# TensorE's completion reports in a graph kernel: on the last matmul, or on a drain behind it

## The reference

```python
# GCN, three times: z1 = conv(x), z2 = conv(z1), z3 = conv(z2)
xw = einsum('ni,tio->tno', x, W)                 # one product per edge type
x_j = xw[edge_type, col] * norm[:, None]         # gather one row per edge, scale it
out = segment_sum(x_j, row, num_segments=N) + b  # add it to the edge's node
z = leaky_relu(out, 0.01)
# GAT, once
alpha = leaky_relu(a_src[src] + a_dst[dst], 0.2)
e = exp(alpha - segment_max(alpha, dst)[dst])
msg = (e / segment_sum(e, dst)[dst])[:, :, None] * xp[src]   # gather again
out = segment_sum(msg, dst)
```

## Time and profile before

| | |
|---|---|
| Time, median of 3 runs | 11929.52 us (11923.69 to 11931.49) |
| Span of the profiled execution (the page gives no other time of it) | 11925.3 us |
| Busy: PE, PEld | 5307.0 us (45%), 4105.0 us (34%) |
| Busy: DVE, ACT | 4574.2 us (38%), 3992.0 us (33%) |
| Busy: POOL | 6395.8 us (54%) |
| First gather of GCN, last gather of GCN | 691.5 us, 8375.1 us |
| First gather of GAT, last gather of GAT | 8505.5 us, 11826.8 us |
| DMA share | 0.1 to 0.2 of the 16 engines |

### The profile page before, as it was taken

The page is one execution under the profiler, slowest core; times in us unless marked ns, Lnnn a source line. Parts: engine busy times, 40 slices in busy tenths (PEclk is TensorE's granted clock), DMA queues, the critical chain, the costliest instruction groups (busy, mean ns, idle before and its releaser), DMA issues.

```text
span 11925.3 us, 149378 instructions
## 1 busy us (share of the span) xinstructions
PE 5307.0 (45%) x32765; PEld 4105.0 (34%) x32766; DVE 4574.2 (38%) x12940; ACT 3992.0 (33%) x12236; POOL 6395.8 (54%) x6521
## 2 busy tenths in 40 slices
PE   5843434434533434343433434343444444444444
PEld 4632322223322323232322323232344444444444
DVE  9952222222322212222322222222555555555556
ACT  6522222222322222222322222222455454445455
POOL 1656566565456565656466565656344444444443
PEclk9975655656655655565655556555566666666666
DMA  1011111111221111111211111111122222222222
GB/s 47 35 42 43 41 44 43 41 44 41 65 55 44 40 44 40 44 40 44 76 42 44 40 44 40 44 40 44 49 69 70 68 71 69 69 68 69 70 69 65
DMA packets 432687, 612.42 MB, mean 51 GB/s; under 512 B 232038, under 2 KB 249491, under 8 KB 432539
## 3 DMA queue, kind: packets, MB, share of 16 engines
q0 software_dynamic: 208832, 428.96, 13.7%
q1 hardware_dynamic: 223707, 182.02, 4.6%
HBM read 437.29 MB, written 51.28 MB: 41 GB/s over the span
## 4 chain that ended last, share of the span: by engine, by line
another core or an unknown queue 48%; DVE 16%; issue 15%; PE 8%; ACTq 5%; DVEq 4%; ACT 3%; POOL 0%; DMA 0%; POOLq 0%; SPq 0%
DVEq L1604 3%; PE bank L1196 3%; ACT g_step L912 3%; ACTq L896 2%; DVE a_miss L1717 2%; PE wide L1196 2%; DVE g_hot L1620 2%; ACTq L912 1%; DVE acc L1634 1%; DVE a_max L1722 1%; DVE lo_hot L1262 1%; DVE acc L1788 1%; PE bank L1191 1%; DVE v_hot L1387 1%
## 5 line engine op out<-in xcount | busy, mean ns | idle before, releaser
L737 POOL DMA_INDIRECT g_rows<-gcn_table,rec_idx x4743 | 4487.1, 946 | 2894.2 <-ACT g_step L912 1484.6
L912 ACT ACTIVATE g_step<-g_rows,rec_w 128x128 f32 x5580 | 1791.5, 390 | 5679.7 <-remote 4618.4
L762 POOL DMA_INDIRECT a_roll<-gat_table,src_plane x1612 | 1524.6, 946 | 1801.0 <-ACT a_cand L937 1375.4
L1634 DVE TENSOR_TENSOR acc<-acc,bank 128x512 f32 x930 | 637.9, 686 | 3828.8 <-remote 3238.9
L1191 PE MATMUL bank<-zeros 1*128 1x512 bf16 x930 | 490.9, 528 | 2909.9 <-DVE acc L1634 2104.6
L1196 PE MATMUL bank<-g_step,g_hot 128*128 128x128 f32 x7440 | 1621.7, 386 | 128.4 <-issue 50.6
L1196 PEld LDWEIGHTS bank<-g_step,g_hot 128*128 128x128 f32 x7440 | 1391.8, 280 | 487.9 <-issue 487.9
L1222 PE MATMUL bank<-a_msg,a_hot 128*128 128x130 f32 x3608 | 798.9, 389 | 1648.7 <-DVE a_msg L1768 1635.0
L1222 PEld LDWEIGHTS bank<-a_msg,a_hot 128*128 128x128 f32 x3608 | 685.6, 283 | 1786.3 <-DVE a_msg L1768 1452.3
L1191 PEld LDWEIGHTS bank<-zeros 1*128 1x128 bf16 x930 | 89.9, 97 | 3099.0 <-DVE acc L1634 2163.3
L937 ACT ACTIVATE a_cand<-a_miss,a_rows 128x128 f32<-128x128 bf16 x3608 | 1095.9, 386 | 14.9 <-DMA a_rows<-a_roll 8.8
(11 more groups left out here) (272 smaller groups left out, 5880.3 us busy)
## 6 DMA issues: line engine op xcount, KB each, us to landing
a_rows<-a_roll SPq DMA_DIRECT2D x451, 264.0 KB
g_rows<-gcn_table,rec_idx POOLq DMA_INDIRECT x4743
gcn_table<-rows SPq DMA_DIRECT2D x147, 256.0 KB
a_roll<-gat_table,src_plane POOLq DMA_INDIRECT x1612
e_dst<-by_dst_dst SPq DMA_DIRECT2D x451, 2.0 KB
gat_table<-acc SPq DMA_DIRECT2D x7, 462.0 KB
out_x<-xs SPq DMA_DIRECT2D x6, 448.0 KB
gcn_slots<-nothing SPq DMA_DIRECT2D x4, 468.0 KB, 6.8
```

The costliest lines, as they stand in the source:

```text
L737: pool.indirect_dma_start(out=g_rows[:, tile % RING, :], out_offset=None, in_=gcn_tables[layer % 2], in_offset=bass.IndirectOffsetOnAxis(a ...
L762: pool.indirect_dma_start(out=a_roll[:, g % ROLL, t, :], out_offset=None, in_=gat_table, in_offset=bass.IndirectOffsetOnAxis(ap=src_plane[ ...
L912: last = nc.scalar.activation(g_step[:, j, k, :].unsqueeze(1), g_rows[:, bass.ds(slots[k], 1), :], ACT.Copy, scale=rec_w[:, bass.ds(q.at(0 ...
L1634: V.tensor_tensor(dst_ap, dst_ap, sums_of(j).rearrange("p (k d) -> p k d", k=GP), ALU.add).then_inc(s_gadd, 1)
```

## The change

First, in the two loops PE no longer adds to `s_gpe`, `sa["T"]`, `sa["pv"]` and `sa["node"]` with the last matmul of each batch. A drain instruction stands behind it, and the drain adds to the semaphore. A drain ends when the engine has finished everything ahead of it. Reports of other matmuls (table products, transposes between layers, the sort) stay on the matmuls.

Second, numbers that are compared with a semaphore are loaded by themselves, with a check that they lie in their range: on ACT the landed tile, on SP the landed group and the slot.

```diff
@@ SP, GAT
-                    _, (tile, slot) = nc.values_load_multi_w_load_instructions(
-                        gat_at[0:1, bass.ds(q.at(0), 1), :].rearrange("p g k -> p (g k)"),
-                        engines=(mybir.EngineType.SP,), min_val=0, max_val=GAT_GROUPS - 1,
-                        skip_runtime_bounds_check_because="a step less the begun blocks, at most the last group")
-                    slot = nc.s_assert_within(slot, 0, ROLL - 1,
-                                              skip_runtime_bounds_check_because="a group modulo the ring")
+                    tile = sp.value_load(gat_at[0:1, bass.ds(q.at(0), 1), 0], min_val=0, max_val=GAT_GROUPS - 1)
+                    slot = sp.value_load(gat_at[0:1, bass.ds(q.at(0), 1), 1], min_val=0, max_val=ROLL - 1)
@@ ACT, GCN
                 def slots_of(q):
+                    tile = act.value_load(gcn_at[32:33, bass.ds(q.at(0), 1), GP], min_val=0,
+                                          max_val=CH * CCOLS - 1)
                     _, values = nc.values_load_multi_w_load_instructions(
-                        gcn_at[32:33, bass.ds(q.at(0), 1), :].rearrange("p g k -> p (g k)"),
-                        engines=(mybir.EngineType.Activation,), min_val=0, max_val=CH * CCOLS - 1,
-                        skip_runtime_bounds_check_because="a step less the begun blocks, at most the last tile")
-                    return values
+                        gcn_at[32:33, bass.ds(q.at(0), 1), 0:GP].rearrange("p g k -> p (g k)"),
+                        engines=(mybir.EngineType.Activation,), min_val=0, max_val=RING - 1,
+                        skip_runtime_bounds_check_because="a tile modulo the ring")
+                    return *values, tile
...
@@ PE, GCN: sum of a group
                                                 g_step[:, j % 3, k, :], start=False, stop=(k == GP - 1))
-                    last.then_inc(s_gpe, 1)
+                    pe.drain().then_inc(s_gpe, 1)
@@ PE, GAT: transposes
-                    last.then_inc(sa["T"], 1)
+                    pe.drain().then_inc(sa["T"], 1)
@@ PE, GAT: messages
-                    last.then_inc(sa["pv"], 1)
+                    pe.drain().then_inc(sa["pv"], 1)
@@ PE, GAT: node values
-                    last.then_inc(sa["node"], 1)
+                    pe.drain().then_inc(sa["node"], 1)
```

More of the change, by code:

```diff
@@ L895, in slots_of @@
                 def slots_of(q):
+                    tile = act.value_load(gcn_at[32:33, bass.ds(q.at(0), 1), GP], min_val=0,
+                                          max_val=CH * CCOLS - 1)
                     _, values = nc.values_load_multi_w_load_instructions(
-                        gcn_at[32:33, bass.ds(q.at(0), 1), :].rearrange("p g k -> p (g k)"),
-                        engines=(mybir.EngineType.Activation,), min_val=0, max_val=CH * CCOLS - 1,
-                        skip_runtime_bounds_check_because="a step less the begun blocks, at most the last tile")
-                    return values
+                        gcn_at[32:33, bass.ds(q.at(0), 1), 0:GP].rearrange("p g k -> p (g k)"),
+                        engines=(mybir.EngineType.Activation,), min_val=0, max_val=RING - 1,
+                        skip_runtime_bounds_check_because="a tile modulo the ring")
+                    return *values, tile
                 def scale(q, values):
                     j = q.slot(0) % 3
-                    *found, tile = values
-                    slots = [nc.s_assert_within(v, 0, RING - 1,
-                                                skip_runtime_bounds_check_because="a tile modulo the ring")
-                             for v in found]
+                    *slots, tile = values
                     if q.live(-3) or layer:
```

## The result

The changed kernel took 12783.45 us (median of 4 runs, 12781.1 to 12819.33), the kernel before 11926.6 us (4 runs, 11923.29 to 11931.49): a ratio of 1.0728, with a 95% interval from 1.0713 to 1.0743. The forecast was 9290 us. The change made the kernel slower by 857 us.

A forecast was written before the change was run, and what follows sets the result against it. It took PE's reports, held while gathers are in flight, to bound the kernel. 11925.3 - 1485 (GCN) + 45 (batches at layer ends) - 1200 (GAT) = 9285, so 9290 us for the median; range 9140 to 12,100.

The forecast's parts named there:

- What bounds the kernel now: GCN and GAT gather loops: PE's reports are held while gathers are in flight; DVE and ACT idle over 4600 us each.
- the circle: Gather loops: POOL gathers until its ring fills, reports held; after it stops they come, ACT scales, slots free, POOL gathers again.
- my sum: Gather loops after release: GCN loses POOL's 1484.6 us of waiting for ACT; GAT takes 2120 us, a gain of 1200.
- If a drain's report is sent at once, the circle breaks: Drains in both loops: each loop then runs at its slowest engine's pace; full release had chance 0.68, at 9290 us.
- its sign of being wrong in this way: Gather loops: "remote" waits as long as now, with drains many us long while POOL gathers.
- My argument against this rival: GCN, against the drain being held too: three held reports arrive one right behind another, as if queued and ready.
- The drain is held as well, slower: Rival, chance 0.12: drain and PE stand while the report is held; GCN +1100 to +1700 us, GAT +400, time 13,700.
- ACT's second load ... the gathers hide it: ACT in GCN: net 0.45 us a group, at most 2.9 us in all, hidden below POOL's 4.34 us.
- SP's loads, "nothing": SP's second load: about 0.6 us a step, ahead of waits ending 5 us apart, so no cost.
- A sequencer's addition is not held there: GCN, against a rival (0.11) of reports late whoever sends: ACT, needing POOL's `s_land`, starts 0.1 us after DVE.

The follow-up runs named there:

- Set 2: Four kernels on chip 15 (kernel before 8942.95 us): one load 8943.18 us, narrow gathers 9130.51, plain copies 8462.06, waiting for landed gathers 11818.26.
- silent drain: Changed kernel with the four reports back on the last matmul and a drain that reports nothing behind each batch: 12810.32 us, 1.0736 of the kernel before.
- set 1: The change taken apart on chip 14 (kernel before 11931.05 us): loads alone 12185.93 us, with GCN drains 12705.49, with GAT drains 12263.69, report plus drain 12810.32.
- set 3: Repeats on chip 11 (kernel before 11921.82 us): changed kernel 12776.21 us, ACT's five numbers in one load with reports on matmuls 11953.2, plain copies 9756.59.
- landing wait after each four: Changed kernel, POOL waiting after each run of four GCN gathers until they have landed: 13058.56 us on chip 8, 11818.26 on chip 15.
- loads only: Changed kernel with all four reports back on the last matmul, leaving only the range-checked loads: 12185.93 us, 1.0215 of the kernel before.
- plain kernel: Changed kernel with GCN's indirect gathers replaced by plain copies of 128 consecutive rows: 9756.59 us on chip 11, 8462.06 on chip 15.

## Why the prediction was wrong

**"What bounds the kernel now": right.** Reports of PE are late while gathers run, DVE and ACT stand until they come, and POOL's ring closes the circle. Set 2 shows it from the other side: where no report is late the circle is gone, with GCN at 6105 us and GAT at 2013, where my sum had 6200 and 2120.

**"If a drain's report is sent at once, the circle breaks": this step failed.** I had read the lateness as something between a finished array and the semaphore, which a sequencer could get round. The drains show that the array, as the chip counts it, is not finished: they last up to 23.9 us behind products whose rows end after 2, which the prediction had named as its sign of being wrong in this way. And the silent drain of set 1 shows that the loss is PE's standing still, whoever reports. The Trainium skill (PSUM — Partial Sum Buffer, Engine vs sequencer instructions) has it as the kernel before had it: put the increment on the matmul, since it fires on completion, while a drain waits for the engine to be wholly idle. I had set the first half against the trace; by the long drains the trace agrees with both halves, and the end of a matmul's row, which is modelled, was the weak witness. My argument against this rival, that three held reports arrive close together, is what one late completion in front of an ordered row of finished ones looks like too.

**The rival "The drain is held as well, slower" was right in its mechanism and too large.** It had a chance of 0.12. I gave +1100 to +1700 us for GCN; it grew by 730 in all, loads included. I had let PE lose two groups in each of 213 cycles, though the earlier trace rows count 191 waits. And the cycles became shorter: POOL waits for ACT 289 times, not 191, and gathers 4836 / 289 = 16.7 tiles between two waits, not 25.3. My reading, which no run tests, is that ACT, let on by the same reports, is held after fewer groups, so there is less work for PE to lose. In GAT, +97 against the +400 that I gave.

**"ACT's second load ... the gathers hide it": wrong.** Its durations were right (0.273 + 0.900 us), but gathers are no cover while ACT's sequencer is slow beside them. Alone it costs some 225 us; beside the drains only 42, since ACT then waits for PE anyway. SP's loads, "nothing", and ACT's two register instructions cost 31 us together in set 3 and nothing in set 2 (8943.18 us against 8942.95).

**"A sequencer's addition is not held there"** stands: in the changed kernel ACT's scaling waits for POOL's additions to `s_land` 55 times, 133.0 us together. It just does not carry over to a sequencer that must first wait for the array.

**Settled and open.** Shown: on the chips that hold, the cause is POOL's indirect DMA instruction, repeated for over 6 us at 1.25 us each; not its bytes, its addresses or the landing of its transfers; a pause of 1.1 us after each four gathers cuts the holds to 3 us, one of 2.4 us removes them, one of 0.7 does neither. Not shown: whether the pause or the lower pace does it, whether the products themselves come late or only the array's word that they are done, what in the chip is occupied by it, why chips 8, 11, 13 and 14 hold and chip 15 did not, and whether the slowed ACT sequencer and the late array are one thing. They come and go together: ACT's longest address instruction takes 0.7 to 1.4 us in every kernel in which drains or reports of GCN are late, and 88 ns on chip 15, with plain copies and with the landing wait after each four. That is a coincidence of place, not a shown cause.

```profile
L907 ACTq FUSED_REGOPS  x5580: 2/74/1414, 823.4 to 8725.5; - x200
```

```profile
L907 ACTq FUSED_REGOPS  x5580: 46/74/88, 750.4 to 6226.1; - x200
```

The first row is of "loads only", the second of the plain kernel on chip 11.

## What to carry to other kernels

A wait that ends "remote", behind an instruction whose modelled row has long ended, can mean that the instruction is not complete, as here; moving the report to a drain turns a late report into a stopped engine. Before costing a fix, test by one edit whether the source of the disturbance can be interrupted: here 1 us of other work on the disturbing engine after each four gathers was worth 5.7%, where changing the reports cost 7.3%. And work laid under a disturbance is not always hidden by it: ACT's separate load cost some 225 us.

## What of the hardware was not expected

- One and the same kernel took 8942.95 us on one chip and, by medians, 11921.82 to 12056.28 us on four others; on each chip its times agree within 0.3%.
- On those four, back-to-back indirect gathers of GpSimd (0.944 us each, 0.30 us apart) keep TensorE's matmuls from being reported complete for up to 24 us from some 6 us into a run until 2.7 to 3.0 us after its last gather; plain copies by the same engine (0.537 us each, runs of up to 39 us) do not.
- In the same stretches ACT's sequencer takes about 0.7 us for an address instruction in place of 0.07 (loads only).
- Where nothing holds them, a drain behind eight passes of 128x128 f32 products ends with the products (1.9 us from hand-over to end). It still keeps PE's sequencer from the next batch: GAT took 2127 and 2161 us with drains and 2011 without on chip 15.
- On ACT a register load of one number takes 0.27 us, of four 0.90, of five 1.12 (medians).
